# Six of each chunk's 26 one-hot tiles made on ScalarE instead of VectorE

## What is computed

```python
edge_index = jnp.stack([src, dst])
h = jnp.maximum(_layernorm(x, axis=-1), 0.0)
# first layer
head = h[edge_index[0]]
tail = h[edge_index[1]]
rel = relation_emb[edge_type]
att_scores = jax.nn.sigmoid(jnp.concatenate([head, rel], axis=-1) @ att_w + att_b)
aggr_emb = jax.ops.segment_sum(att_scores * tail, edge_index[0], num_segments=6250)
x = x + jnp.tanh(aggr_emb @ W_w.T + W_b)
# second layer: attention over the same edges, softmax by edge_index[0]
```

## Time and profile before

| | us |
|---|---|
| median of 3 runs | 5862.91 (5853.55 to 5887.29) |
| the profiled execution | 5865.56 |
| its span in the profile | 5863.7 |
| the chunks of `relation_layer` | about 412 of it (2878 to 3290) |
| TensorE, VectorE, ScalarE busy in those 412 | 353.71, 378.17, 104.59 |

### The profile page before, as it was taken

One profiled execution on the slowest core, in us unless ns is written; L12 is line 12 of the kernel. 1 busy time (PEld: TensorE's weight loads), 2 busy tenths in 40 slices (PEclk: granted clock), 3 DMA queues, 4 the chain that ended last, 5 costly groups with the idle time before them and its releaser, 6 DMA issues. The chain is left out here.

```text
span 5863.7 us, 79660 instructions
## 1 busy us (share of the span) xinstructions
PE 2726.4 (46%) x21110; PEld 1693.1 (29%) x21111; DVE 3881.4 (66%) x8751; ACT 2758.0 (47%) x5413; POOL 3278.9 (56%) x3388
## 2 busy tenths in 40 slices
PE   7655555555555555555488622322223222222223
PEld 7433333333333333333388511111111111111102
DVE  9867777777777777776599645655556666655552
ACT  3244444444444444444122345655555555555552
POOL 0146565666666565656610266666666666666653
PEclk8555555555555555555577755555555555555555
DMA  5112121212121212121477533433334343433321
GB/s 64 55 54 71 63 71 62 71 63 71 63 71 63 71 63 71 63 71 58 103 160 145 72 103 100 124 110 108 108 103 111 109 110 103 110 108 109 109 79 24
DMA packets 691304, 505.28 MB, mean 86 GB/s; under 512 B 588446, under 2 KB 605214, under 8 KB 691109
## 3 DMA queue, kind: packets, MB, share of 16 engines
q1 hardware_dynamic: 573012, 246.99, 18.2%
q0 software_dynamic: 108736, 196.93, 11.6%
q10 hardware_dynamic: 9360, 59.56, 2.7%
HBM read 289.96 MB, written 213.26 MB: 86 GB/s over the span
## 5 line engine op out<-in xcount | busy, mean ns | idle before, releaser
L625 POOL DMA_INDIRECT records<-rec,place x1612 | 1557.2, 966 | 1306.9 <-issue 451.0
L1395 POOL DMA_INDIRECT got_a<-kv_table,idx_a x1612 | 1539.5, 955 | 762.8 <-issue 691.9
L860 DVE SCALAR_TENSOR_TENSOR same_before<-p_src,src_f,before 128x128 bf16<-128x128 f32 x1612 | 775.0, 535 | 0.0
L711 ACT ACTIVATE lo_away<-p_lo,minus_number 128x512 bf16<-128x512 f32 x434 | 291.2, 671 | 615.5 <-remote 593.6
L668 PE MATMUL p_src<-fields,select 3*128 3x512 bf16 x434 | 248.3, 572 | 687.7 <-DVE same_before L860 512.0
L1411 PE MATMUL p_a<-ident,flat_attr 128*128 128x128 f32 x434 | 123.5, 433 | 930.5 <-issue 447.4
L807 DVE TENSOR_TENSOR picked<-p_look,hi_hot 128x392 f32<-128x392 f32 x434 | 231.5, 533 | 407.5 <-remote 398.2
L1420 PE MATMUL p_a<-relu,w_t 128*128 128x512 f32 x248 | 230.8, 1034 | 463.4 <-issue 332.5
L850 DVE TENSOR_SCALAR dst_hot<-p_dst,number 128x512 bf16<-128x512 f32 x434 | 307.3, 708 | 191.1 <-remote 178.1
L643 PE MATMUL p_look<-table_low,lo_hot_t 128*128 128x98 bf16 x1612 | 410.2, 281 | 0.0
L643 PE MATMUL p_look<-table_rest,lo_hot_t 128*128 128x98 bf16 x1612 | 409.4, 280 | 0.0
(11 more groups left out here) (377 smaller groups left out, 8443.3 us busy)
## 6 DMA issues: line engine op xcount, KB each, us to landing
sums<-packed_a ACTq DMA_DIRECT2D x62, 936.0 KB
q_starts<-zero_q SPq DMA_DIRECT2D x62, 884.0 KB
rec_r<-records SPq DMA_DIRECT2D x124, 442.0 KB
qin<-q_starts SPq DMA_DIRECT2D x62, 884.0 KB
attr_a<-records SPq DMA_DIRECT2D x62, 442.0 KB
records<-rec,place POOLq DMA_INDIRECT x1612
got_a<-kv_table,idx_a POOLq DMA_INDIRECT x1612
stage<-in_edge_attr SPq DMA_DIRECT2D x61, 416.0 KB
```

The source lines that it names most:

```text
L625: nc.gpsimd.indirect_dma_start(k.records, bass.IndirectOffsetOnAxis(ap=place[b][:, t:t + 1], axis=0), rec[b][:, t, :], None).then_inc(s_se ...
L711: nc.scalar.activation(lo_away[qb][:, 0:m * P], p_lo[:, 0:m * P], ACT.Abs, bias=k.minus_number[:]).then_inc(s_lo_away, 1)
L860: last = v.scalar_tensor_tensor(same_before[:, first:first + j + 1, :].rearrange("p g e -> p (g e)"), p_src[:, 0:(j + 1) * P], k.src_f[:, ...
L1395: nc.gpsimd.indirect_dma_start(got[b][:, t, :], None, k.kv_table, bass.IndirectOffsetOnAxis(ap=idx[b][:, t:t + 1], axis=0)).then_inc(s_got ...
```

## The change

VectorE's `lo` instruction now covers only the first 20 tiles of a chunk (`SHARE = 20`). ScalarE makes the others, 6 in a chunk of 26 and 4 in a chunk of 24, one by one behind its cast: an `Abs` of `rel - iota_p` into a 128 x 128 fp32 tile `away`, and a `Relu` of `1 - away` into the column of `lo`. The second waits for the first through a semaphore, `s_away`. VectorE computes the row numbers of those tiles a second time in fp32 (`rel_last`), since ScalarE takes its bias in fp32, before it raises `s_in`. TensorE waits for a new semaphore, `s_lo`, ahead of tile 20.

```diff
+SHARE = 20
+        rel_last = [tile(f"rel_last{b}", [P, T - SHARE]) for b in range(2)]
+        away = [tile(f"away_r{b}", [P, P]) for b in range(2)]
+        s_away, s_lo = sem("s_away_r"), sem("s_lo_r")
 ...
                     for t in range(tiles):
+                        if t == SHARE:
+                            pe.wait_ge(s_lo, n + 1)
                         for part in (high[b][:, t, :], mid[:, t, :, 1], low[b][:, t, :]):
 ...
                     nc.scalar.copy(high[b][:, 0:tiles, :], of[:, :, H0:REC]).then_inc(s_high, 1)
+                    for t in range(SHARE, tiles):
+                        done = ...
+                        nc.scalar.activation(away[t % 2][:], k.iota_p[:], ACT.Abs, bias=rel_last[b][:, t - SHARE:t - SHARE + 1], scale=-1.0).then_inc(s_away, 1)
+                        act.wait_ge(s_away, done + 1)
+                        last = nc.scalar.activation(lo[b][:, :, t], away[t % 2][:], ACT.Relu, bias=k.ones[:, 0:1], scale=-1.0)
+                    if tiles > SHARE:
+                        last.then_inc(s_lo, 1)
 ...
+                    if tiles > SHARE:
+                        c.mark(v.tensor_tensor(rel_last[b][:, 0:tiles - SHARE].rearrange("p (s e) -> p s e", e=SUPER), of[:, SHARE:tiles, SRC].rearrange("p (s e) -> p s e", e=SUPER),
+                                               bc(base[:, SHARE // SUPER:tiles // SUPER], 2, SUPER), ALU.subtract))
                     c.wait()
                     dve.sem_inc(s_in, 1)
-                    c.mark(v.tensor_tensor(lo[b][:, :, 0:tiles], k.iota_b[:, :, 0:tiles], bc(rel[b][:, 0:tiles], 1, P), ALU.is_equal))
+                    own = min(tiles, SHARE)
+                    c.mark(v.tensor_tensor(lo[b][:, :, 0:own], k.iota_b[:, :, 0:own], bc(rel[b][:, 0:own], 1, P), ALU.is_equal))
```

More of the change, by code:

```diff
@@ L1042, in copy @@
                     nc.scalar.copy(high[b][:, 0:tiles, :], of[:, :, H0:REC]).then_inc(s_high, 1)
+                    for t in range(SHARE, tiles):
+                        done = (n if not isinstance(n, int) or n < CHUNKS else CHUNKS) * (T - SHARE) + (max(n - CHUNKS, 0) * (tiles2 - SHARE) if isinstance(n, int) else 0) + t - SHARE
+                        nc.scalar.activation(away[t % 2][:], k.iota_p[:], ACT.Abs, bias=rel_last[b][:, t - SHARE:t - SHARE + 1], scale=-1.0).then_inc(s_away, 1)
[3 more added lines that the diff above has]
+                        last.then_inc(s_lo, 1)
                 def body(i):
@@ L1057, in _ @@
                 v = nc.vector
-                c = Chain(dve, s_dve, 2 * 2)
+                c = Chain(dve, s_dve, 2 * 3)
                 v.memset(zeros[:], 0.0).then_inc(s_zero, 1)
@@ L1081, in way @@
                 def way(slow):
-                    c.per_turn = 6 if slow else 4
+                    c.per_turn = 8 if slow else 6
                     c.fewer = 0
```

## The result

| | before | after |
|---|---|---|
| median of the runs | 5862.91 us (3 runs) | 5946.32 us (3 runs, 5927.10 to 5953.24) |
| the profiled execution | 5865.56 | 5927.10 |
| its span | 5863.7 | 5925.3 |

The ratio is 1.0143, with a 95% interval of 1.0109 to 1.0178. Run again on another chip, where the kernel before takes 5029.08 us and repeats within 0.1%, it was 1.0187 (1.0173 to 1.0201), 94.5 us. The forecast was 5900 us, with a range of 5857 to 5928.

The account below looks back on a forecast made before the run. VectorE and TensorE were taken as tied at 12.35 us a turn of two chunks; ScalarE at 6.79 us a chunk would then set the pace, +38 us over 62 chunks, giving 5900 us, range 5857 to 5928.

Parts of the forecast that it names:

- The Relu: ScalarE's write into a column of `lo`: 0.40 us compact plus 1.15 ns x 128 = 0.15 us, so 0.55 us.
- the upper end of 0.66: Longest Relu allowed for: 2.0 ns x 128 more than compact, from a small pair of column writes, 0.66 us.
- the slower case: By the cacheline note, each access to a new 16-byte line pays a penalty, so the change comes out slower; no figure for writes.
- The tile: One Abs and Relu pair on ScalarE: 0.40 + 0.04 + 0.45 = 0.89 us, likely range 0.80 to 0.95 us.
- The cast: ScalarE's copy making `high` ahead of its six tiles, said to block 1.48 us a chunk.
- The chunk: ScalarE's work for one chunk: 1.48 + 5.31 = 6.79 us, above 6.176, so it sets the pace; upper end 7.48 us.
- VectorE's side: `lo` 0.40 us shorter, but `rel_last` and the wait for `high` take it back: net -0.04 us a chunk, -0.1 to +0.05.
- TensorE's side: The stop for `s_lo` ahead of tile 20 costs only its own instruction, 0 to 0.15 us a chunk, hidden behind ScalarE.
- The 12.09 us floor: TensorE's own time for a turn of two chunks, limiting any gain to 8 us, 0.14% of the time.
- A: Rival: column writes are hidden or free, ScalarE just fits at 0.74 us a tile, 5855 to 5866 us; chance 0.25.
- C: Rival: ScalarE fits, but `rel_last` and the break at tile 20 eat the gap, 5863 to 5871 us; chance 0.10.
- B: Rival: column writes cost in full, nothing hides, 1.00 us a tile, 7.48 us a chunk, 5944 us; chance 0.10 with beyond.

Follow-up runs that it names:

- e4_widths: Kernel before plus a quiet stretch of 128-element writes, ten in a row: ScalarE bf16 at step 26 starts every 0.57 us, fp32 at step 13 every 0.29 us.
- e3_vector_side: Changed kernel, but ScalarE makes no tile, the six columns stay zero and TensorE skips `s_lo`: 6.13 us a chunk behind the start, ratio 0.9991 to before.
- e9_nobody: Kernel before, plus six Abs and spread Relu on ScalarE behind each cast, into a tile nobody reads: 7.67 us a chunk, ratio 1.0135.
- e1_compact: Changed kernel, but ScalarE's Relu writes each one-hot compactly into its own tile: 6.02 us a chunk behind the start, ratio 0.9973 to before.
- e5_one_relu: Changed kernel, but six Abs write fp32 columns and one Relu writes runs of six bf16: 6.12 us a chunk, ratio 0.9987 to before.

## Why the prediction was wrong

The direction was right, and so was who pays: ScalarE became the engine that sets the pace, and `rest` waits for its `high`. The sum was not. The step that failed is "I take 1.15 ns x 128 = 0.15 us, a Relu of 0.55 us": it priced a column of lone bf16 by rows of fp32. The Relu took 0.88 us, and what it still had to write held up the instruction behind it. Of ScalarE's 7.70 us a chunk against 6.79, the six tiles make 0.59 us and the cast 0.32; the 62 chunks cost 92.8 us against 38.

- **The Relu.** Measured 0.88 us, above even the upper end of 0.66. Both prices came from fp32 rows: the strided reads of the earlier trace rows and the column writes of the earlier trace rows. e4_widths shows that fp32 writes take at most 0.50 us at any step and bf16 ones 1.06. The type of the element was the missing term, and no row of the trace before had a lone bf16 write. The fp32 price was itself too high: 0.49 us at 400 bytes is 0.8 ns an element over compact, not the 2.0 read from 26 elements. The note on SBUF cachelines of the Trainium skill ("SBUF — State Buffer"), quoted for the slower case, points the right way for bf16, but by it two elements 52 bytes apart are in different lines whatever their type, and here fp32 writes at that distance follow each other as closely as compact ones; the measurement decides.
- **The tile.** Predicted 0.40 + 0.04 + 0.45 = 0.89 us, measured 1.01 to 1.04 from the second on (0.98 on average). Its parts differ: the next Abs starts 0.38 us after the Relu, sooner than thought, but then takes 0.60 to 0.63. The earlier trace rows had shown that overlap, and the prediction read it as the cost being hidden. It is hidden only until something waits for the end of the next instruction, and here the dependent Relu does.
- **The cast.** Predicted to block 1.48 us, measured 1.80, held up by the last Relu's writes. This was not in the sum: 0.32 us x 62 = 20 us.
- **The chunk.** 1.80 + 5.90 = 7.70 us against 6.79. The upper end in the text, 7.48 us, was too low too.
- **VectorE's side.** Right: `lo` 1.49 us, `rel_last` 0.1 us, a late `high`, nearly nothing in sum (e3_vector_side: 0.05 us a chunk). One reading of the start was off: the 12.13 us that VectorE was said to need for a turn on its own hold a gap of 0.19 us. In about a quarter of the turns of the kernel before, the second chunk took 5.97 us like the first, and the turn 11.95:

```profile
2977.26 0.20 DVE L1069 TENSOR_TENSOR rel<-rec_r,base 128x26 bf16<-128x26 f32 x1 [0.59 <-PE acc L1014]
...
2989.21 0.20 DVE L1069 TENSOR_TENSOR rel<-rec_r,base 128x26 bf16<-128x26 f32 x1
```

  So TensorE's 12.09 us were the longer of the two already, which fits that a shorter `lo` gained next to nothing.
- **TensorE's side.** Right that the stop at tile 20 costs nothing (e9_nobody has the same pace without it). The 12.09 us floor was right for this layout; the prediction did not see that compact tiles lower it.
- **Rivals.** A and C fell with the Relu's length. B named the tile nearest to the truth, 1.00 us, and got 0.10, but by luck: it added a Relu of 0.66 us and an Abs of 0.40 with almost no overlap, where the trace has 0.88 and 0.61 overlapping by half a microsecond.

## What to carry to other kernels

When work is moved to an idle engine, read the shape that it writes there, element type and step together, and if no row has that shape, leave the upper bound open rather than borrow it from another type. On ScalarE, in the shapes measured here, do not write single bf16 elements more than 8 bytes apart: write two on end, write fp32 and pack it in one instruction, or write compactly and let the reader take two layouts. An instruction that starts early behind a slow one has not hidden it if something waits for its end.

## What else the runs showed of the hardware

- **TensorE came to a crawl at the start of the loop in some runs.** In e1_compact single matmuls stood 0.7 to 2.8 us apart for about 50 us in the first turns, with no wait that the profile names, and the second and third interval from `rel` to `rel` were 14.3 and 44.0 us, 46 us too many:

```profile
2994.56 0.21 PE L1022 MATMUL acc<-low,lo_r 128*128 128x64 bf16 x1 [2.58 <-issue]
2996.66 0.21 PE L1022 MATMUL acc<-high,lo_r 128*128 128x64 bf16 x1 [1.89 <-issue]
```

  The same happened in e3_vector_side's profile (again 46 us) and in none of the other ten. Its cause was not tried. The runs of the kernel before on that chip spread from 5837 to 5950 us; whether such a stretch is part of that spread is not known. It is why those two paces are counted behind the start.
- **The kernel before took medians of 5863 to 5900 us in three sets of runs and 5029 in a fourth, on another chip.** The pace of the chunks did not go with it: the changed kernel has 7.67 us on the 5029 us chip and on the first. Of the changed kernel's 5925.3 - 5127.5 = 798 us between two profiles 538 lie ahead of the first `rel` (2860.7 against 2322.5), in the sorting stage, and the rest behind the chunks. A gain is best measured where the chip repeats: there e5_one_relu's 0.13% could be told.
- **VectorE pays for lone bf16 writes too, but less:** 0.27 us a piece in a row at step 26 against 0.16 us for fp32 at step 13, both 52 bytes apart (e4_widths, ten on end):

```profile
3444.12 3.09 DVE L1889 TENSOR_SCALAR vec_half<-iota_p 128x128 bf16<-128x128 f32 x10 [48.67 <-ACT got_full L1906]
3446.73 1.70 DVE L1891 TENSOR_SCALAR vec_full<-iota_p 128x128 f32<-128x128 f32 x10
```
